# A reordered front of a one-core decoder kernel: activations loaded first, half of the tokens projected first, convolution in place

## The reference

```
h      = x * rsqrt(mean(x*x) + eps) * ln1_w            # 1024 tokens x 512
zxbcdt = h @ w_in.T                                     # 512 z, 128 xs, 128 Bs, 512 Cs, 4 dt
xBC    = silu(causal_depthwise_conv4(xs|Bs|Cs) + conv_b)
dt     = softplus(dt + dt_bias);  a = dt * -exp(A_log);  cs = cumsum(a) per sequence
Ldec   = exp(cs_q - cs_k), lower triangle
Y      = ((Cs Bs^T) * Ldec) @ (xs*dt) + D * xs;  out = (Y * silu(z)) @ w_out.T
```

## Time and profile before

| | us |
|---|---|
| three runs: median (lowest to highest) | 433.87 (432.69 to 434.31) |
| span of the profiled execution | 432.9 |
| PE busy | 417.5 (96%) |
| DVE busy | 211.8 (49%) |
| ACT busy | 161.4 (37%) |
| POOL busy | 67.6 (16%) |

### The profile page before, as it was taken

How to read it: one execution, slowest core, us unless ns; L and a number is a source line. 1 busy time by engine, 2 the same in 40 slices (tenths; PEclk the granted TensorE clock), 3 DMA queues, 4 the chain that set the end, 5 groups by cost and what they waited for, 6 DMA issues and landing times.

```text
span 432.9 us, 5328 instructions
## 1 busy us (share of the span) xinstructions
PE 417.5 (96%) x1966; PEld 331.7 (77%) x1966; DVE 211.8 (49%) x392; ACT 161.4 (37%) x327; POOL 67.6 (16%) x51
## 2 busy tenths in 40 slices
PE   7999999999999999999999999999999999999984
PEld 2788887766667888888888888888787887887763
DVE  1586996135774431212122222254366576576566
ACT  5636655555653521212121212243232232241221
POOL 2412222344292110101010202020000000000000
PEclk9799999999999999999999999999999999999998
DMA  7610210020020021212121212111101201201001
GB/s 218 246 50 2 91 55 28 22 97 2 0 98 2 2 97 48 97 48 97 48 97 48 97 48 97 48 50 48 48 2 48 74 24 49 73 24 51 24 0 73
DMA packets 10256, 25.67 MB, mean 59 GB/s; under 512 B 1696, under 2 KB 1824, under 8 KB 10240
## 3 DMA queue, kind: packets, MB, share of 16 engines
q1 hardware_dynamic: 9088, 23.36, 16.1%
q10 hardware_dynamic: 1152, 2.10, 1.3%
HBM read 23.36 MB, written 2.10 MB: 59 GB/s over the span
## 4 chain that ended last, share of the span: by engine, by line
PE 88%; DVE 5%; ACT 3%; issue 1%; DMA 1%; SPq 0%; ACTq 0%; DVEq 0%
PE bank L338 25%; PE bank L339 25%; PE bank L340 25%; PE bank L394 2%; PE bank L382 2%; PE bank L546 2%; PE bank L535 1%; DMA rows<-x 1%; PE bank L557 1%; PE bank L403 1%; DVE tmp L1087 1%; PE bank L424 1%; PE bank L349 1%; PE bank L527 1%; PE bank L441 1%
## 5 line engine op out<-in xcount | busy, mean ns | idle before, releaser
L338 PE MATMUL bank<-cols,ringS 128*128 128x512 f32 (+1 forms) x328 | 126.6, 386 | 1.4 <-DVE cols L937 1.3
L340 PE MATMUL bank<-cols,ringS 128*128 128x512 f32 (+1 forms) x328 | 124.5, 380 | 0.0
L339 PE MATMUL bank<-cols,ringS 128*128 128x512 f32 (+1 forms) x328 | 124.5, 380 | 0.0
L338 PEld LDWEIGHTS bank<-cols,ringS 128*128 128x128 f32 x328 | 62.1, 189 | 15.0 <-issue 2.9
L339 PEld LDWEIGHTS bank<-cols,ringS 128*128 128x128 f32 x328 | 62.1, 189 | 11.8 <-issue 0.5
L340 PEld LDWEIGHTS bank<-cols,ringS 128*128 128x128 f32 x328 | 61.9, 189 | 11.6
L1054 DVE TENSOR_TENSOR big<-tmp,bank 128x512 f32 (+1 forms) x28 | 19.3, 688 | 102.2 <-ACT tmp L798 102.2
L338 PE MATMUL bank<-wdS,cols 128*128 128x512 f32 x144 | 61.4, 427 | 0.0
L340 PE MATMUL bank<-wdS,cols 128*128 128x512 f32 x144 | 56.4, 392 | 0.0
L339 PE MATMUL bank<-wdS,cols 128*128 128x512 f32 x144 | 56.2, 390 | 0.0
L798 ACT ACTIVATE tmp<-bank 128x512 f32<-128x512 f32 x28 | 16.8, 598 | 105.6 <-PE bank L340 105.6
(11 more groups left out here) (134 smaller groups left out, 513.2 us busy)
## 6 DMA issues: line engine op xcount, KB each, us to landing
raw<-wstream SPq DMA_DIRECT2D x31, 512.0 KB, 3.2
rows<-x SPq DMA_DIRECT2D x8, 256.0 KB, 4.6
big<-ctxT SPq DMA_DIRECT2D x8, 256.0 KB, 2.6
big<-ctx SPq DMA_DIRECT2D x8, 256.0 KB, 2.9
out<-tmp ACTq DMA_DIRECT2D x8, 256.0 KB, 2.0
big<-ln_w SPq DMA_DIRECT2D x2, 256.0 KB, 5.4
big<-lora_b SPq DMA_DIRECT2D x3, 64.0 KB
ga<-gate_lora SPq DMA_DIRECT2D x1, 72.0 KB
```

Of the source, the lines that this page charges most:

```text
L338: pe.matmul(ps, a_hi, b_lo, start=first, stop=False)
L339: pe.matmul(ps, a_hi, b_hi, start=False, stop=False)
L340: return pe.matmul(ps, a_lo, b_hi, start=False, stop=last)
```

## The change

It is confined to the part before the scores. In words, by engine:

- SP issues tile 0, one 2 KB row of `ln1_w`, tiles 1 to 3, chunks 0 and 1, tiles 4 and 5, four small constants (own semaphore `taps_in`), tiles 6 and 7, chunk 2, and the other seven constants.
- PE spreads `ln1_w` over the partitions by a matmul of a row of ones into bank 7, and DVE's `norm1` reads it there. Zero matmuls: 10, then 4 after tiles 0 and 1, and 4 after tiles 2 and 3, none later. PE waits for the first three steps of POOL's setup instead of all eight.
- `IN_ORDER` is now (0,0), (1,0), (2,0), (3,0), (0,1), (1,1), (2,1), (3,1) and then as before. Only the first product is in two parts. Tiles 4 and 5 are transposed after product 1, tiles 6 and 7 after product 2.
- Chunk 0 is split in two halves of 512 columns, each with its own high and low part.
- ACT makes the squares of tile 6 ahead of the high part of tile 4 and those of tile 7 ahead of the high part of tile 5; DVE puts the first convolution ahead of the low parts of tiles 6 and 7.
- The last tap, the three taps and the silu all write the place of the result; the two accumulators and the wait for them go.
- ACT computes |v + bias| from PSUM, DVE only max(v + bias, 0): one DVE step a half instead of three, one ACT step more. Both softplus halves come ahead of all silu.
- POOL's preparation of `lora_b` moves from behind chunk 0 to behind chunk 2.

```diff
-IN_ORDER = ((0, 0), (1, 0), (0, 1), (1, 1)) + tuple((m, hf) for m in range(2, N_IN) for hf in range(2))
+IN_ORDER = tuple((m, hf) for hf in range(2) for m in range(4)) \
+    + tuple((m, hf) for m in range(4, N_IN) for hf in range(2))
...
+            load_rows(0, 1)
+            sp.dma_start(ln1row, ln1_w.partition_broadcast(1)).then_inc(ln1_in, 16)
+            load_rows(1, HB)
             load_chunk(0)
+            load_chunk(1)
+            load_rows(HB, HB + 2)
+            for dst, src in ((alog[:, :], a_log), (dtb[:, :], dt_bias), (cw[:, :, :], conv_w), (cb[:, :], conv_b)):
+                sp.dma_start(dst, src).then_inc(taps_in, 16)
+            load_rows(HB + 2, B)
+            load_chunk(2)
...
+            keep_warm(10, *zeros)
+            pe.wait_ge(vec_setup, 1)
+            pe.wait_ge(ln1_in, 16)
+            pe.matmul(bank[LN1_BANK][:, :], ones[0:1, :], ln1row, start=True, stop=True).then_inc(ln1_ps, 1)
+            pe.wait_ge(pool_setup, 3)
             turn_h(0)
             turn_h(1)
+            keep_warm(4, *zeros)
             turn_h(2)
+            turn_h(3)
+            keep_warm(4, *zeros)
             in_proj(0, 2, 0)
             in_proj(0, 2, 1)
+            in_proj(1)
             turn_h(4)
             turn_h(5)
+            in_proj(2)
             turn_h(6)
             turn_h(7)
+            in_proj(3)
...
             norm1(0, 2)
             norm1(2, HB)
             hi_of_hT(0)
             hi_of_hT(1)
+            first_hi(0)
             hi_of_hT(2)
+            first_hi(1)
+            act.sem_inc(w_hi, 1)
+            hi_of_hT(3)
+            ring_hi(1)
             norm1(HB, HB + 2)
+            norm1_squares(HB + 2, HB + 3)
+            hi_of_hT(HB)
+            norm1_squares(HB + 3, B)
+            hi_of_hT(HB + 1)
+            rms(0, HB + 2, B, sq1, lr1, rs1)
+            act.wait_ge(taps_in, 16 * N_TAPS)
             conv_last_tap(0)
+            hi_of_hT(HB + 2)
+            hi_of_hT(HB + 3)
             act.activation(expa[:, :], alog[:, :], ACT.Exp).then_inc(expa_ok, 1)
+            softplus_abs(0)
             softplus(0)
+            conv_last_tap(1)
+            conv_last_tap(2)
+            softplus_abs(1)
             softplus(1)
+            conv_last_tap(3)
+            ring_hi(2)
+            for i in range(3):
+                conv_silu(i)
+            for i in range(4, 2 * N_CONV):
                 conv_last_tap(i)
                 conv_silu(i - 1)
+                if i in (5, 9):
                     ring_hi(2 + i // 4)
...
+            for t in range(HB, HB + 2):
+                norm1(t)
+            for t in range(HB, HB + 2):
+                low1(t)
+            for t in range(HB + 2, B):
+                norm1(t)
             conv_taps(0)
+            low1(HB + 2)
+            low1(HB + 3)
+            softplus_relu(0)
+            for i in range(1, 2 * N_CONV):
+                if CONV_ORDER[i] == (1, 1):
+                    softplus_relu(1)
                 conv_taps(i)
```

More of the change, by code:

```diff
@@ L232, in _ @@
                 sp.dma_start(dst, src).then_inc(const_in, 16)
[L233 to L236, removed]
             for n in range(RAW, LOOP_CHUNK):
@@ L283, in lo_part @@
                 pool.tensor_tensor(dst, raw[:, raw_slot(n), :], hi.bitcast(F32), ALU.subtract).then_inc(w_lo, 1)
-            for n in range(IN_CHUNKS):
+            for q in range(2):
+                q_ = bass.ts(q, D)
+                pool.wait_ge(w0_hi, q + 1)
+                pool.tensor_tensor(ringS[:, 0, 1, q_], raw[:, raw_slot(0), q_], ringS[:, 0, 0, q_].bitcast(F32),
+                                   ALU.subtract).then_inc(w0_lo, 1)
+            pool.wait_ge(w0_lo, 2)
+            pool.sem_inc(w_lo, 1)
+            for n in range(1, IN_CHUNKS):
                 lo_part(n, ringS[:, n % 2, 1, :], ringS[:, n % 2, 0, :])
-                if n == 0:
+                if n == 2:
                     pool.wait_ge(const_in, 16 * N_CONST)
@@ L332, in conv_product, with conv_out @@
         def conv_product(i):
-            return IN_ORDER.index((1 + i // 2, i % 2))
+            return IN_ORDER.index(CONV_ORDER[i])
+        def conv_out(i):
+            m, h_ = CONV_ORDER[i][0] - 1, half(CONV_ORDER[i][1])
+            return xT[:, h_] if m == 0 else bT[:, h_] if m == 1 else cT[:, m - 2, h_]
         def three_pass(pe, ps, a_hi, a_lo, b_hi, b_lo, first, last):
@@ L355, in in_proj @@
                 width = HALF // parts
-                pe.wait_ge(w_lo, m // 2 + 1)
+                if m < 2:
+                    pe.wait_ge(w0_lo, m + 1)
+                else:
+                    pe.wait_ge(w_lo, m // 2 + 1)
                 pe.wait_ge(hT_lo, HB * hf + (part + 1) * HB // parts)
@@ L680, in norm1 @@
                     squares(0, t, rows[:, t, :], sq1)
+            def norm1(t0, t1):
+                norm1_squares(t0, t1)
                 if t0 == 0:
@@ L687, in hi_of_hT, with softplus_abs @@
                 act.activation(token_cols(t, 0), blocks(bank[t % 2][:, :]), ACT.Copy).then_inc(hT_hi, 1)
+            def softplus_abs(hf):
+                n = IN_ORDER.index((0, hf))
+                act.wait_ge(ip_done, n + 1)
+                act.activation(negcs[:, half(hf)], bank[IN_BANK[n]][0:H, :], ACT.Abs, bias=dtb[:, 0:1]) \
+                    .then_inc(sp_abs, 1)
             def softplus(hf):
                 v = negcs[:, half(hf)]
-                act.wait_ge(sp_step, 3 * (hf + 1))
-                act.activation(v, v, ACT.Exp).then_inc(sp_exp, 1)
+                act.wait_ge(sp_abs, hf + 1)
+                act.activation(v, v, ACT.Exp, scale=-1.0).then_inc(sp_exp, 1)
                 act.wait_ge(sp_exp, hf + 1)
@@ L742, in _, with first_hi @@
             act.preload_act_table_set(LN_EXP)
+            def first_hi(q):
+                q_ = bass.ts(q, D)
+                act.wait_ge(raw_in[raw_slot(0)], 16)
+                act.activation(ringS[:, 0, 0, q_], raw[:, raw_slot(0), q_], ACT.Copy).then_inc(w0_hi, 1)
             norm1(0, 2)
```

125 lines of the change are left out of this document (47 added, 78 removed).

## The result

Over the executions shown, the kernel after has a median of 430.85 us (8 executions, 429.69 upwards) against 433.69 us before (8, 432.69 to 434.85). The ratio is 0.9932, 95% interval 0.9912 to 0.9951: faster by 0.7%. One of the eight executions of the kernel after took 703.59 us at a mean clock of 0.561, which is rival 5 carried to its extreme and which no trace explains; it is in that median, and left out of the ratio and of all that follows. The other seven have a median of 430.27 us and spans of 427.7, 427.8, 428.1, 428.3, 429.5, 429.5 and 430.2 us. The profiled one has a span of 427.8 us and a time of 429.73, so 1.9 us lie around the span, not the 1.0 that I had taken from the median.

What follows compares the result with a forecast made beforehand. PE bounds the kernel, busy without a gap from product 4, which starts at 28.55 instead of 31.53 us: 432.9 - 3.0 = 429.9 of span, plus 1.0 around it, 430.9 us; range 427.8 to 433.6.

Steps and rivals of the forecast that it cites:

- rival 5: Front and first products: the clock stays low; gain used up if until 22.2 us, 434.8 us if until 24; chance 0.09.
- the 1.0 that I had taken from the median: Around the profiled span: 1.0 us between the span and the median of the runs, added to 429.9.
- The load of `ln1_w`: Front: without the 128-partition broadcast, x tiles 1 to 3 land about 2 us earlier.
- the chain from tile 4 through ACT and DVE: Ahead of product 4: from tile 4 turned at 20.9, ACT and DVE work sets product 4's start at 28.55 us.
- Behind product 4 nothing is given back: After product 4: edits cost DVE or ACT, not PE, so the 3.0 us gained in front stays.
- rival 1: Front: the clock doesn't fall, product 4 starts at 26.0, gain 5.5 us, 428.4 us; chance 0.22.
- Product 0: at the low clock until 16.15, 2.45 us: Product 0: 11 matmuls at low clock in 2.45 us, then 13 at 0.126 each, ending at 17.7 us.
- Rival 2: Front: tiles don't land earlier, tile 2 still at 7.87 us; gain 1.9 us, 432.0 us; chance 0.12.
- Rival 3: Softplus on ACT: Abs needs its own table loads, 5.1 us in all, product 8 waits 1.2, 432.1 us; chance 0.05.
- Rival 4: Gain given back: chunk 2's slack gone, or ACT-DVE chain ahead of product 4 2 us longer; 433 us; chance 0.10.
- chunk 2's slack: Ahead of product 8: chunk 2 ready at +9.6 us after product 4's start, product 8 at +10.9, slack 1.3 us.
- the move of the softplus: After product 4: DVE has 2.7 us less work, Abs on ACT costs about 0.7 but is covered; nothing booked.

Runs made afterwards that it cites:

- the control: The kernel after, unchanged, measured again beside three other experiments on one chip: 429.93 us, ratio 0.9917 to the kernel before.
- the three clock runs: Kernel after without eight zero matmuls: 430.97 us; kernel before with PE's gaps filled by more: 433.83 us; kernel after with its gaps filled: 430.04 us.
- the silu experiment: Kernel after with the first two convolutions' silus ahead of the second softplus half on ACT, two more table loads: 430.49 us, ratio 0.9928.

## Why the prediction was right, and where it was not

**The mechanism** was right in three parts. The load of `ln1_w` was the thing in front: with it back the median is 2.4 us above the control's (432.37 against 429.93), and its removal alone gives 1.6. The new bound ahead of product 4 is the chain from tile 4 through ACT and DVE: high part 19.03 to product 4 at 26.32, 7.3 us, against 28.55 - 20.9 = 7.65 forecast, with its waits of 0.3 and 0.4 ahead of tiles 6 and 7 and of product 4 found at 0.14 ahead of tile 6 (22.16 behind a matmul of 21.78, less 0.24) and 0.27 between the two tiles (1.31 - 1.04), and at 0.25 (26.32 behind a matmul of 25.84, less 0.23). Behind product 4 nothing is given back.

**The size** was wrong by the clock. I had product 0 start at 13.7 and run at 1.2 GHz until 16.15. In the profiled run the clock didn't fall (rival 1, 5.5 us, against 5.2 measured), and in the control it was low from 8.6 to 12.0, was back before product 0, and cost some 0.3 us. The failed term is "Product 0: at the low clock until 16.15, 2.45 us": in both traces product 0 runs at the full level throughout. The pattern that I forecast is that of the run without zero matmuls, which has product 4 at 27.54. The rule of the Trainium skill, "TensorE: Matmul & The Clock Gate", section "HAM oscillation — how this bites in real kernels", that idle gaps drop the clock and work without them keeps it, agrees with the three clock runs (0.50 with gaps, 1.00 with them filled). It doesn't tell the traces of the kernel after and of its control apart, which idle alike and of which one kept the clock.

**The base** was wrong too. I took the gain from one profiled execution, 432.9 us of span, where 23 executions of the kernel before on one chip have 431.0 to 433.4 with a median of 431.8: the profiled one had a long fall of the clock (mean 0.988), which only 4 of its 50 other executions have. And I took 1.0 us around the span, where it is 1.95. So 432.9 - 3.0 + 1.0 = 430.9 has a base 1.1 too high, a gain about 0.5 too low (431.8 to 428.3, the median of the seven, is 3.5), and 0.95 too little around: 431.8 - 3.5 + 1.95 = 430.25. That the number was met is luck in good part: these offset one another, and the long eighth execution lifts the median from 430.27 to 430.85. Of the 5.1 us between the two traces about 1.4 is the fall in the one before, an estimate from 432.9 less the 431.5 of the executions with 0.996 or more.

**Rival 2** (tiles not earlier) was a part of the truth: tile 2's squares moved from 7.87 to 5.60, tile 3's only from 8.68 to 7.25, after 0.95 us of waiting for x. **Rival 3** fell: no table load around the Abs, which takes 0.67 us, as the page "ScalarE: Activation LUTs" of the Trainium skill, section "Table sets: the hidden batching unit", had it. **Rival 4** is the one that the experiments filled with content. I had named chunk 2's slack as 1.3 us; it is 1.0, and it is the place that breaks: silu ahead of the second softplus half takes it and 0.24 more, the softplus on DVE takes it and 4.9 more. I had booked the move of the softplus at nothing ("since ACT is covered") and its 2.7 us on DVE as slack. The sum came out right, but the reason misses what the move is for: left on DVE at its place, the softplus holds up ACT by waits of the two for each other, which no sum of work shows. **Rival 5** (clock low to 22) didn't occur in any trace; the highest span of the seven, 430.2, stays below the lowest of before on any chip, 430.5.

**Left open:** which front the executions with 429.5 and 430.2 us of span had. Traces of other kernels suggest one whose clock rises late (next section but one) for the first two, with mean clocks of 0.996; the mean clock of 0.990 of the third suggests a fall. But no execution of the kernel after itself was profiled in it.

## What to carry to other kernels

Where one engine is busy nearly all the time, find the point from which it never idles and ask only when that point is reached; here 401.4 us behind it didn't move in any version that kept its chunk in time. Price a moved step not by its length but by who waits behind it: 2.7 us of DVE work in the wrong place of the queue cost 6.8 us between two traces. And take the base from the spans of many executions, not from the profiled one, before a gain of under 1% is worked out: see first whether the profiled one's mean clock is that of most of them.

## What the runs showed of the hardware

A broadcast load of one 2 KB row into 128 partitions holds up the loads behind it. From 3.5 to 6 us the three traces with it have 129, 177 and 229 GB/s (at 0.80, 0.55 and 0.83 busy), the eleven with the row alone 264 to 315; the squares of tile 2 start at 7.53 to 7.87 with it and at 5.60 to 6.98 without.

The clock column reads 1.00 at the very beginning even where the matmuls take about twice their time. PE of the silu experiment, in order of time:

```profile
5.68 2.07 PE L483 MATMUL bank<-tmp,ones 1*128 1x512 f32 x2
8.69 1.94 PE L375 MATMUL bank<-ident,tmp 128*128 128x128 f32 x8 [0.93 <-DVE tmp L986]
10.42 1.91 PE L475 MATMUL bank<-big 128*128 128x512 bf16 x4
```

These are nearly twice the 1.28, 1.22 and 1.03 above, up to 12 us, under a column of 1.00 (the clock of its stretches from 5 to 8, 8 to 12 and 12 to 14 us): the rise from the low level comes at another moment in each execution, near 5 us in the run with filled gaps and after 12 us here, though PE's list up to the ones matmul is the same. The profiled spans of kernels with this late rise are 428.6 (squares early, without the four zero matmuls), 429.9 (silu early), 431.4 (the row alone) and 433.9 us (old order), the upper groups of their own executions. In the kernels of the new order these groups lie 1.5 to 2 us apart. So the length of one instruction of known price, not the column, tells the clock at the front of a kernel.
